# In plain heads of attention, the first addition of probabilities on VectorE instead of GpSimd

## The chip, the core and the metric

The kernel runs on one core of a Trainium2 chip. The metric is the device time of one execution in microseconds. Three runs of the kernel before took 2719.68 to 2723.65 us, with a median of 2723.48. TensorE (PE) does the matmuls, PEld in a profile is its loading of weights, VectorE is DVE, ScalarE is ACT, GpSimd is POOL, and SP issues the transfers.

## What is computed

The input is `x` of 8 x 1024 x 512 numbers in float32. A block of attention with 8 heads of 64 dimensions is followed by a feed-forward block. Cut to what matters:

```
h  = layernorm(x)
q, k = h @ W_qk + b_qk          # per head, interleaved
v  = h @ W_v + b_v
attn = softmax(q k^T * 64**-0.5)
o  = attn @ v
x  = x + (layernorm(o @ W_out + b_out) * gamma + beta + h) * 2**-0.5
x  = x + sigmoid(xr @ W_r^T) * (relu(xk @ W_k^T)**2 @ W_v^T)
```

`xr` and `xk` mix each row of the second layernorm with the row before it. The change concerns the softmax alone: the sum of the exponentials over the keys.

## The kernel before

The first pass (`attention_pass`) works through 8 batches of 8 heads, 64 heads in all, written out head by head; the second pass does the rest from about 1945 us on. A head has 1024 queries and 1024 keys. Keys are taken in 8 tiles of 128 (`TT`). The work of a head `h` is:

- **Scores and exponents.** `scores` (lines 788 to 802) makes for key tile j a block of 128 keys x 1024 queries in one of two areas `ps_st`, ScalarE's `exponent` (617 to 623) writes `probs[:, j, :]` from it. The maximum of each query is subtracted by an extra row in the matmul, so it must be known before the scores.
- **Row maxima.** They are taken a head ahead. `rows` (763 to 781) makes, for head h+1, 16 blocks of 128 queries x 512 keys, j = 0 to 15, in turn in the two areas `ps_max`; VectorE's `reduce_max` (412 to 418) reduces each block and increments `max_done`. Block j may be written only when the maximum of block j-2 has been taken (line 779). `join_max` joins them, `turn_max` (line 786, one per head) turns them into a row.
- **Sums.** The 8 tiles of `probs` are added up in `acc` by seven additions of 128 x 1024 numbers, `add_probs` (314 to 324) on GpSimd: the first is probs 0 + probs 1 (line 320), the other six add one tile each (line 324). Then `sum_rows` (817 to 824) sums over the partitions with a matmul of ones (line 822). It stands at the start of the next head on TensorE, behind `p_at_v` for the last four tiles (line 812) and ahead of `turn_max`.
- **The product with v and the rest.** `p_at_v` (line 812) multiplies probs by v. GpSimd normalises the result and splits it (lines 330 and 335), two heads later, ahead of its additions.
- **Projections** of q and k for the heads to come (`project_qk`, line 739) are put between the blocks above.

Each engine has a list of steps written out by hand, and semaphores between them. Heads differ by their place in the batch (`h % 8`). Places 1 to 5 are plain heads on all engines (place 5 has some more steps on ScalarE and GpSimd), place 0 carries projections of v, places 6 and 7 prepare the next batch. On TensorE, the middle of a plain head is:

```
scores(b, h, 0, 1)
rows(b, h + 1, 3, 4)
scores(b, h, 1, 3)
rows(b, h + 1, 4, 6)
scores(b, h, 3, 4)
rows(b, h + 1, 6, 8)
...
project_qk(b, h + 2, 0, 0, 4)
scores(b, h, 4, 5)
```

and on VectorE the maxima of the next head are taken with the reciprocal of the sums (`invert_sums`) of the head before between them.

Of the kernel before, what the change touches and what calls it, by code (L numbers as in the profile page):

```python
# [19 lines left out]
ALU = mybir.AluOpType  # L20
# [5 lines left out]
HEADS, DH = 8, 64  # L26
KC = C // P
TT = T // P
# [18 lines left out]
def rows_of(j):  # L47

    if j < 8:
        return j % 4, j // 4  # L50
    return 4 + (j - 8) // 2, j % 2


def attention_pass(nc, x, w_qk, b_qk, w_v, b_v, w_out, w_r, spare, stage, o_hi_scratch, o_lo_scratch, inv_scratch, ln1_stats,
                   ident):
    with ExitStack() as ctx:
        def sb(name, shape, dt=F32):
            return ctx.enter_context(nc.sbuf_tensor(name, shape, dt))

        def sem(name):  # L60
            return ctx.enter_context(nc.semaphore(name))
# [18 lines left out]
        probs = sb("probs", [P, TT, T])  # L80
        acc = sb("acc", [P, T])
# [82 lines left out]
        exp_done = sem("exp_done")  # L164
        acc_done = sem("acc_done")
        sum_done = sem("sum_done")
# [27 lines left out]
        with nc.Block() as block:  # L194
# [92 lines left out]
            def _(pool):  # L287
# [9 lines left out]
                def rstd_of(b):  # L297
                    pool.wait_ge(bn_done, b)
                    pool.tensor_tensor(rstd[:, :], mean_var[:, :, 1], eps[:, :], ALU.add).then_inc(eps_done, 1)
                    pool.wait_ge(eps_done, b)  # L300
                    pool.tensor_tensor(shift[:, :], mean_var[:, :, 0], neg_one[:, :], ALU.mult).then_inc(shift_step, 1)
                    pool.tensor_tensor(rstd[:, :], rstd[:, :], neg_half[:, :], ALU.pow).then_inc(rstd_step, 1)
                    pool.wait_ge(shift_step, b)
                    pool.wait_ge(rstd_step, b)
                    pool.tensor_tensor(shift[:, :], shift[:, :], rstd[:, :], ALU.mult).then_inc(rstd_done, 1)
# [8 lines left out]
                def add_probs(b, h, j):  # L314

                    if j == 1:
                        if h >= 1:
                            pool.wait_ge(sum_done, 8 * b + h)
                        pool.wait_ge(exp_done, 64 * b + 8 * h + 2)
                        pool.tensor_tensor(acc[:, :], probs[:, 0, :], probs[:, 1, :], ALU.add).then_inc(acc_done, 1)  # L320
                    else:
                        pool.wait_ge(exp_done, 64 * b + 8 * h + j + 1)
                        pool.wait_ge(acc_done, 56 * b + 7 * h + j - 1)
                        pool.tensor_tensor(acc[:, :], acc[:, :], probs[:, j, :], ALU.add).then_inc(acc_done, 1)  # L324

                def normalise_o(b, h):

                    pool.wait_ge(o_copied, 8 * b + h + 1)
                    pool.wait_ge(inv_in, 256 * b + 32 * h + 32)
                    pool.tensor_tensor(oT[h % 2][:, :], oT[h % 2][:, :], inv_cols[:, :], ALU.mult).then_inc(o_done, 1)  # L330

                def split_o(b, h):

                    pool.wait_ge(oT_hi_done, 8 * b + h + 1)
                    pool.tensor_tensor(oT[h % 2][:, :].bitcast(F32R), oT[h % 2][:, :], oT_hi[h % 2], ALU.subtract).then_inc(oT_lo_done, 1)  # L335
# [10 lines left out]
                def head(b, h, last):  # L346
                    if h >= 2:
                        normalise_o(b, h - 2)
                        split_o(b, h - 2)
                    if h == 5 and not last:  # L350
                        rstd_of(b + 1)
                    for j in range(1, TT):
                        add_probs(b, h, j)

                head(0, 0, False)
                head(0, 1, False)
                for b in range(B - 1):
                    for h in range(2, HEADS + 2):
                        head(b, h, False)
# [7 lines left out]
            def _(dve):  # L367
# [5 lines left out]
                def stats(b, t):  # L373
                    dve.wait_ge(x_in[t // 2], 16 * b + 16)
                    dve.bn_stats(bn6[:, t, :], xb[:, t, :]).then_inc(bn_step, 1)

                def aggregate():
                    for t in range(TT):
                        ins = dve.bn_aggr(mean_var[:, t, :], bn6[:, t, :])
                    ins.then_inc(bn_done, 1)  # L380
# [18 lines left out]
                def store_qk_lo(b, h, half, ps=ps_misc):  # L399
                    dve.wait_ge(qk_hi_done, 16 * b + 2 * h + half + 1)  # L400
                    cols = slice(half * HALF, (half + 1) * HALF)
                    i, hd = h % 2, h % HEADS
                    dve.scalar_tensor_tensor(kA[i][0:DH, cols], ps[DH:P, :], bqk[DH:P, hd:hd + 1],  # L403
                                             f32(kA[i][DH:P, cols]), ALU.add, ALU.subtract).then_inc(k_lo_done, 1)
                    dve.scalar_tensor_tensor(qB[i][0:DH, cols], ps[0:DH, :], bqk[0:DH, hd:hd + 1],
                                             f32(qA[i][0:DH, cols]), ALU.add, ALU.subtract).then_inc(q_lo_done, 1)
# [5 lines left out]
                def reduce_max(b, h, first, end):  # L412

                    for j in range(first, end):
                        r, kh = rows_of(j)
                        dve.wait_ge(rows_done, 128 * b + 16 * h + j + 1)
                        dve.tensor_reduce(half_max[:, r, kh:kh + 1], ps_max[(j + 1) % 2][:, :], AX_X,  # L417
                                          ALU.max).then_inc(max_done, 1)

                def join_max(b, h):  # L420

                    dve.wait_ge(max_done, 128 * b + 16 * h + 16)
                    dve.tensor_reduce(neg_max[:, :], half_max[:, :, :], AX_X, ALU.max, negate=True).then_inc(neg_max_done, 1)

                def invert_sums(b, h):
                    dve.wait_ge(sums_in, 256 * b + 32 * h + 32)
                    dve.reciprocal(inv_sq[:, :], sums_sq[:, :]).then_inc(recip_done, 1)
# [32 lines left out]
                reduce_max(0, 0, 12, 16)  # L460
                join_max(0, 0)

                def plain_head(b, h, last):
                    place = h % HEADS
                    extra = not last
                    if extra and place == 5:
                        dve.wait_ge(bn_step, 8 * b + 16)
                    store_qk_lo(b, h + 1, 0)
                    if extra and 2 <= place <= 4:
                        for t in range(3 * place - 6, min(3 * place - 3, TT)):  # L470
                            stats(b + 1, t)
                    if extra and place == 5:
                        aggregate()
                    reduce_max(b, h + 1, 0, 3)
                    store_qk_lo(b, h + 1, 1)
                    reduce_max(b, h + 1, 3, 4)
                    if h >= 1:
                        invert_sums(b, h - 1)
                    reduce_max(b, h + 1, 4, 16)
                    join_max(b, h + 1)  # L480

                def late_v_head(b, h):
# [53 lines left out]
                def head(b, h, last):  # L536
                    place = h % HEADS
                    if place == 0:
                        late_v_head(b, h)
                    elif place == 6 and not last:  # L540
                        turning_head(b, h)
                    elif place == 7 and not last:
                        early_v_head(b, h)
                    elif place == 7:
                        invert_sums(b, h - 1)
                    else:
                        plain_head(b, h, last)
# [1004 lines left out]
```

## Time and profile before

| | us |
|---|---|
| median of 3 runs | 2723.48 |
| the profiled execution, its time | 2721.03 |
| its span, from the first to the last instruction | 2719.2 |
| PE busy | 2625.8 (97%) |
| PE loads busy | 1782.0 (66%) |
| DVE busy | 1631.3 (60%) |
| POOL busy | 1521.1 (56%) |
| ACT busy | 1290.6 (47%) |

Busy times are unions of the recorded instructions. Matmuls are pipelined and their ends are modelled, so that two of them overlap in the record: what counts is the time from one start to the next. In a row of the time line, like instructions that follow each other closely are merged (x2, x6), and the brackets give the idle time of the engine before the row and what ended it.

### The profile page before, as it was taken

What the parts mean: (1) busy time and instruction counts of PE and PEld (TensorE: products, weight loads), DVE (VectorE), ACT (ScalarE), POOL (GpSimd) and SP (SyncE); (2) the same over time, 40 slices, a digit from 0 to 9 for tenths busy, and PEclk for the clock granted to TensorE, in tenths of its full rate; (3) what the DMA queues carried; (4) which work ended last, traced back from release to release, by engine and by line L of the source; (5) the groups of instructions that cost most, each with busy time, mean ns of one, the idle gap of its engine ahead of it and who ended that gap; (6) DMA issues with size and microseconds to landing.
All of it is one profiled execution on the core that took longest, in us unless ns stands there. A gap on an engine that the chain in (4) does not pass through costs nothing. (4 is left out here: it accounts for less than half of the span.)

```text
span 2719.2 us, 31997 instructions
## 1 busy us (share of the span) xinstructions
PE 2625.8 (97%) x11376; PEld 1782.0 (66%) x11376; DVE 1631.3 (60%) x2679; ACT 1290.6 (47%) x1833; POOL 1521.1 (56%) x819
## 2 busy tenths in 40 slices
PE   6999999999999999999999999999579999999999
PEld 5655656665565666556556666665358888888887
DVE  7555455456545545654554555455278787878785
ACT  3345346335534634553463455344245555555554
POOL 3576477567647756764775676577323333333333
PEclk9999999999999999999999999999779999999999
DMA  2222122122112212211221221122322222222220
GB/s 97 63 47 51 36 78 53 42 71 55 44 38 75 55 40 71 57 42 48 66 55 40 70 60 39 40 50 79 122 90 99 85 96 89 93 92 89 96 77 32
DMA packets 108410, 178.32 MB, mean 66 GB/s; under 512 B 22401, under 2 KB 22913, under 8 KB 108289
## 3 DMA queue, kind: packets, MB, share of 16 engines
q1 hardware_dynamic: 108288, 176.75, 22.5%
q8 instruction: 71, 1.16, 0.2%
q14 instruction: 51, 0.41, 0.0%
HBM read 92.02 MB, written 50.59 MB: 52 GB/s over the span
## 5 line engine op out<-in xcount | busy, mean ns | idle before, releaser
L417 DVE TENSOR_REDUCE half_max<-ps_max 128x1 f32<-128x512 f32 x1024 | 680.3, 687 | 549.7 <-PE ps_max L780 543.4
L324 POOL TENSOR_TENSOR acc<-acc,probs 128x1024 f32<-128x1024 f32 x384 | 914.0, 2380 | 157.5 <-ACT probs L623 109.2
L623 ACT ACTIVATE probs<-ps_st 128x1024 f32<-128x1024 f32 x512 | 522.0, 1023 | 591.8 <-PE ps_st L801 589.6
L812 PE MATMUL ps_o<-probs,v 128*64 128x512 f32 x2048 | 467.7, 598 | 0.0
L800 PE MATMUL ps_st<-qA,kA 128*128 128x512 f32 x1024 | 415.3, 406 | 13.9 <-DMA qB<-max_row 9.4
L801 PE MATMUL ps_st<-qB,kB 65*128 65x512 f32 x1024 | 408.2, 399 | 0.0
L780 PE MATMUL ps_max<-kA,qA 128*128 128x512 f32 x1024 | 386.8, 416 | 3.7 <-issue 1.4
L320 POOL TENSOR_TENSOR acc<-probs 128x1024 f32<-128x1024 f32 x64 | 152.8, 2387 | 287.6 <-ACT probs L623 287.6
L812 PEld LDWEIGHTS ps_o<-probs,v 128*64 128x64 f32 x2048 | 135.6, 136 | 265.4 <-issue 236.5
L780 PEld LDWEIGHTS ps_max<-kA,qA 128*128 128x128 f32 x1024 | 188.6, 188 | 138.6 <-issue 63.5
L800 PEld LDWEIGHTS ps_st<-qA,kA 128*128 128x128 f32 x1024 | 194.7, 190 | 82.3 <-ACT probs L623 32.7
L801 PEld LDWEIGHTS ps_st<-qB,kB 65*128 65x128 f32 x1024 | 194.7, 190 | 40.9
L739 PE MATMUL ps_misc<-xT_hi,wqk_lo 128*128 128x512 f32 x508 | 206.4, 406 | 12.8 <-DVE wqk_lo L450 9.3
L335 POOL TENSOR_TENSOR oT<-oT,spare 128x512 fp32r<-128x512 f32 x64 | 82.3, 1286 | 223.4 <-ACT spare L615 223.4
L739 PE MATMUL ps_misc<-xT_lo,wqk_hi 128*128 128x512 f32 x508 | 201.2, 396 | 0.0
L739 PE MATMUL ps_misc<-xT_hi,wqk_hi 128*128 128x512 f32 x508 | 201.0, 396 | 0.0
L591 ACT ACTIVATE kA<-ps_misc,bqk 64x512 fp32r<-64x512 f32 x127 | 86.6, 682 | 205.1 <-PE ps_misc L739 199.5
L410 DVE TENSOR_TENSOR v<-ps_misc,bv 128x512 f32<-128x512 f32 x60 | 41.5, 692 | 186.0 <-PE ps_misc L748 186.0
L403 DVE SCALAR_TENSOR_TENSOR kA<-ps_misc,bqk,kA 64x512 fp32r<-64x512 f32 x127 | 96.0, 756 | 66.3 <-ACT qA L592 66.0
L1453 PE MATMUL bank<-mix_wout_hi,o_lo 128*128 128x512 f32 x256 | 102.8, 402 | 22.5 <-DMA o_lo<-o_lo_scratch 19.1
L597 ACT ACTIVATE max_row<-ps_max 8x128 fp32r<-8x128 f32 x64 | 17.0, 266 | 225.7 <-PE ps_max L786 225.7
L1212 POOL TENSOR_TENSOR rstd_y<-mv_y,eps 128x4 f32<-128x4 f32 x16 | 3.2, 202 | 205.6 <-DVE mv_y L1257 205.6
(174 smaller groups left out, 4629.6 us busy)
## 6 DMA issues: line engine op xcount, KB each, us to landing
stage<-in_L_attn_x_dram SPq DMA_DIRECT2D x32, 512.0 KB, 5.8
qA<-qA SPq DMA_DIRECT2D x128, 128.0 KB, 2.3
kB<-kA SPq DMA_DIRECT2D x128, 128.0 KB, 2.4
o_hi_scratch<-spare SPq DMA_DIRECT2D x128, 128.0 KB, 2.3
o_lo_scratch<-oT SPq DMA_DIRECT2D x128, 128.0 KB, 2.4
o_hi<-o_hi_scratch SPq DMA_DIRECT2D x16, 1024.0 KB, 5.4
o_lo<-o_lo_scratch SPq DMA_DIRECT2D x16, 1024.0 KB, 7.7
xc<-in_L_attn_x_dram SPq DMA_DIRECT2D x16, 1024.0 KB, 5.2
```

Source lines behind the costliest of these rows:

```text
L320: pool.tensor_tensor(acc[:, :], probs[:, 0, :], probs[:, 1, :], ALU.add).then_inc(acc_done, 1)
L324: pool.tensor_tensor(acc[:, :], acc[:, :], probs[:, j, :], ALU.add).then_inc(acc_done, 1)
L403: dve.scalar_tensor_tensor(kA[i][0:DH, cols], ps[DH:P, :], bqk[DH:P, hd:hd + 1], f32(kA[i][DH:P, cols]), ALU.add, ALU.subtract).then_inc(k ...
L417: dve.tensor_reduce(half_max[:, r, kh:kh + 1], ps_max[(j + 1) % 2][:, :], AX_X, ALU.max).then_inc(max_done, 1)
L591: act.activation(kA[i][DH:P, cols], ps[DH:P, :], ACT.Identity, bias=bqk[DH:P, hd:hd + 1])
L623: act.activation(probs[:, j, :], ps_st[j % 2][:, :], ACT.Exp).then_inc(exp_done, 1)
L739: ins = pe.matmul(ps[:, :], w[:, kc, h % HEADS, :, :].rearrange("p s d -> p (s d)"), xt[:, kc, cols], start=(n == 0), stop=(n == 11))
L780: pe.matmul(ps_max[(j + 1) % 2][:, :], qA[h % 2][:, r * P:(r + 1) * P], kA[h % 2][:, kh * HALF:(kh + 1) * HALF], start=True, stop=True).th ...
L800: pe.matmul(ps_st[j % 2][:, cols], kA[h % 2][:, tile], qA[h % 2][:, cols], start=True, stop=False)
L801: ins = pe.matmul(ps_st[j % 2][:, cols], kB[h % 2][:, tile], qB[h % 2][:, cols], start=False, stop=True)
L812: ins = pe.matmul(ps_o[half * DH:(half + 1) * DH, :], v[:, j, hd * DH:(hd + 1) * DH], probs[:, j, half * HALF:(half + 1) * HALF], start=(j ...
L1453: ins = pe.matmul(out, a[:, kc, a_cols], b[:, kc, b_cols], start=(i == 0), stop=(i == len(prods) - 1))
```

## The change

In heads with place 1 to 5, the first addition of probabilities is taken out of GpSimd's list. VectorE does it, into the same `acc`, behind the row maximum of block 4 (the fifth) of the next head. The increments of `acc_done` stay in the same order, so that GpSimd's second addition waits for VectorE's.

```diff
@@ -349,7 +349,8 @@
                         split_o(b, h - 2)
                     if h == 5 and not last:
                         rstd_of(b + 1)
-                    for j in range(1, TT):
+                    first = 2 if 1 <= h % HEADS <= 5 else 1
+                    for j in range(first, TT):
                         add_probs(b, h, j)
 
                 head(0, 0, False)
@@ -460,6 +461,13 @@
                 reduce_max(0, 0, 12, 16)
                 join_max(0, 0)
 
+                def add_first_probs(b, h):
+
+                    if h >= 1:
+                        dve.wait_ge(sum_done, 8 * b + h)
+                    dve.wait_ge(exp_done, 64 * b + 8 * h + 2)
+                    dve.tensor_tensor(acc[:, :], probs[:, 0, :], probs[:, 1, :], ALU.add).then_inc(acc_done, 1)
+
                 def plain_head(b, h, last):
                     place = h % HEADS
                     extra = not last
@@ -476,7 +484,10 @@
                     reduce_max(b, h + 1, 3, 4)
                     if h >= 1:
                         invert_sums(b, h - 1)
-                    reduce_max(b, h + 1, 4, 16)
+                    reduce_max(b, h + 1, 4, 5)
+                    if 1 <= place <= 5:
+                        add_first_probs(b, h)
+                    reduce_max(b, h + 1, 5, 16)
                     join_max(b, h + 1)
 
                 def late_v_head(b, h):
```

VectorE, one plain head (place 1), from the second half of the projections stored to the joined maximum. Before:

```order
L417 TENSOR_REDUCE half_max<-ps_max 128x1 [waits rows_done] x3
L403 SCALAR_TENSOR_TENSOR kA<-ps_misc,bqk,kA 64x512 [waits qk_hi_done]
L405 SCALAR_TENSOR_TENSOR qB<-ps_misc,bqk,qA 64x512
L417 TENSOR_REDUCE half_max<-ps_max 128x1 [waits rows_done]
L427 RECIPROCAL inv_sq<-sums_sq 32x32 [waits sums_in]
L417 TENSOR_REDUCE half_max<-ps_max 128x1 [waits rows_done] x12
L423 TENSOR_REDUCE neg_max<-half_max 128x8 [waits max_done]
```

The same head now:

```order
L418 TENSOR_REDUCE half_max<-ps_max 128x1 [waits rows_done] x3
L404 SCALAR_TENSOR_TENSOR kA<-ps_misc,bqk,kA 64x512 [waits qk_hi_done]
L406 SCALAR_TENSOR_TENSOR qB<-ps_misc,bqk,qA 64x512
L418 TENSOR_REDUCE half_max<-ps_max 128x1 [waits rows_done]
L428 RECIPROCAL inv_sq<-sums_sq 32x32 [waits sums_in]
L418 TENSOR_REDUCE half_max<-ps_max 128x1 [waits rows_done]
L469 TENSOR_TENSOR acc<-probs 128x1024 [waits exp_done,sum_done]
L418 TENSOR_REDUCE half_max<-ps_max 128x1 [waits rows_done] x11
L424 TENSOR_REDUCE neg_max<-half_max 128x8 [waits max_done]
```

The twelve maxima behind the reciprocal have become one, the addition, and eleven.

GpSimd, two successive plain heads: the addition into `acc` and the normalisation and splitting of an earlier head. Before:

```order
L320 TENSOR_TENSOR acc<-probs 128x1024 [waits exp_done,sum_done]
L324 TENSOR_TENSOR acc<-acc,probs 128x1024 [waits acc_done,exp_done] x6
L330 TENSOR_TENSOR oT<-oT,inv_cols 128x512 [waits inv_in,o_copied]
L335 TENSOR_TENSOR oT<-oT,spare 128x512 [waits oT_hi_done]
L320 TENSOR_TENSOR acc<-probs 128x1024 [waits exp_done,sum_done]
```

Now:

```order
L324 TENSOR_TENSOR acc<-acc,probs 128x1024 [waits acc_done,exp_done] x6
L330 TENSOR_TENSOR oT<-oT,inv_cols 128x512 [waits inv_in,o_copied]
L335 TENSOR_TENSOR oT<-oT,spare 128x512 [waits oT_hi_done]
L324 TENSOR_TENSOR acc<-acc,probs 128x1024 [waits acc_done,exp_done] x6
```

The row of line 320 is gone there, and the six others follow the splitting directly. TensorE's, ScalarE's and SP's lists are the same as before.

## Rows read from the trace of the kernel before

**Rows 1.** The page, busy time of each engine (share of the span).

```profile
PE 2625.8 (97%) x11376; PEld 1782.0 (66%) x11376; DVE 1631.3 (60%) x2679; ACT 1290.6 (47%) x1833; POOL 1521.1 (56%) x819
```

**Rows 2.** Waits: who waited for whom, us in total, times, longest us.

```profile
PEld ps_max L780 <- DVE half_max L417: 35.8, 116, 0.4
...
PE ps_max L822 <- POOL acc L324: 6.3, 2, 4.2
```

**Rows 3.** Time line, PEld, start of a plain head (start, duration, instructions).

```profile
567.31 0.08 PEld L786 LDWEIGHTS ps_max<-ident,neg_max 128*8 128x8 f32 x1 [0.81 <-issue]
```

**Rows 4.** Time line, DVE, the same head.

```profile
573.97 0.67 DVE L417 TENSOR_REDUCE half_max<-ps_max 128x1 f32<-128x512 f32 x1
574.57 0.33 DVE L427 RECIPROCAL inv_sq<-sums_sq 32x32 f32<-32x32 f32 x1
574.91 1.29 DVE L417 TENSOR_REDUCE half_max<-ps_max 128x1 f32<-128x512 f32 x2
576.41 1.29 DVE L417 TENSOR_REDUCE half_max<-ps_max 128x1 f32<-128x512 f32 x2 [0.21 <-PE ps_max L780]
```

**Rows 5.** Time line, PEld, the same head: row products 6 and 7.

```profile
575.75 0.19 PEld L780 LDWEIGHTS ps_max<-kA,qA 128*128 128x128 f32 x1
576.26 0.19 PEld L780 LDWEIGHTS ps_max<-kA,qA 128*128 128x128 f32 x1 [0.32 <-DVE half_max L417]
576.37 0.19 PEld L739 LDWEIGHTS ps_misc<-xT_hi,wqk_lo 128*128 128x128 f32 x1
576.60 0.19 PEld L739 LDWEIGHTS ps_misc<-xT_lo,wqk_hi 128*128 128x128 f32 x1
```

**Rows 6.** Time line, POOL, the same head.

```profile
574.60 2.39 POOL L320 TENSOR_TENSOR acc<-probs 128x1024 f32<-128x1024 f32 x1 [3.87 <-ACT probs L623]
...
577.13 14.98 POOL L324 TENSOR_TENSOR acc<-acc,probs 128x1024 f32<-128x1024 f32 x6
592.08 1.27 POOL L330 TENSOR_TENSOR oT<-oT,inv_cols 128x512 f32<-128x512 f32 x1
```

**Rows 7.** Time line, PEld, where this head ends and the next begins.

```profile
591.49 0.14 PEld L812 LDWEIGHTS ps_o<-probs,v 128*64 128x64 f32 x2 [0.28 <-issue]
592.23 0.26 PEld L822 LDWEIGHTS ps_max<-acc,ones 128*64 128x64 f32 x4 [0.60 <-issue]
593.30 0.08 PEld L786 LDWEIGHTS ps_max<-ident,neg_max 128*8 128x8 f32 x1 [0.81 <-issue]
```

**Rows 8.** Time line, PEld, the end of a head of place 0.

```profile
802.12 0.14 PEld L812 LDWEIGHTS ps_o<-probs,v 128*64 128x64 f32 x2 [0.28 <-issue]
802.55 0.14 PEld L822 LDWEIGHTS ps_max<-acc,ones 128*64 128x64 f32 x2 [0.29 <-issue]
...
803.94 0.08 PEld L786 LDWEIGHTS ps_max<-ident,neg_max 128*8 128x8 f32 x1 [0.81 <-issue]
```

**Rows 9.** Time line, PEld, start and end of a head with a longer gap.

```profile
1828.59 0.08 PEld L786 LDWEIGHTS ps_max<-ident,neg_max 128*8 128x8 f32 x1 [0.81 <-issue]
...
1853.80 0.23 PEld L822 LDWEIGHTS ps_max<-acc,ones 128*64 128x64 f32 x4 [0.89 <-issue]
1854.83 0.08 PEld L786 LDWEIGHTS ps_max<-ident,neg_max 128*8 128x8 f32 x1 [0.81 <-issue]
```

**Rows 10.** Time line, ACT, the head of rows 3 to 7: its first two exponents.

```profile
572.38 2.07 ACT L623 ACTIVATE probs<-ps_st 128x1024 f32<-128x1024 f32 x2
```

**Rows 11.** Groups by line and form, DVE: count, busy us, mean ns, idle before.

```profile
L1292 DVE TENSOR_TENSOR mr_lo<-stage,mr_hi 128x512 fp32r<-128x512 f32 x64 | 40.8, 700 | 0.0
...
L1292 DVE TENSOR_TENSOR mk_lo<-stage,mk_hi 128x512 fp32r<-128x512 f32 x64 | 39.8, 685 | 0.0
...
L1296 DVE TENSOR_TENSOR mix_wout_lo<-stage,mix_wout_hi 128x2048 fp32r<-128x2048 f32 x1 | 2.3, 2292 | 8.6 <-ACT mix_wout_hi L1389 8.6
```

**Rows 12.** One line's instructions, second pass: duration ns min/median/max, first and last start.

```profile
L1286 DVE SCALAR_TENSOR_TENSOR stage<-lnT,mu_r,stage x64: 736/743/1781, 1998.4 to 2685.2; 128x512 f32<-128x512 f32 x64
```

**Rows 13.** Windows: length, busy us (x instructions) by engine, granted clock, DMA share, GB/s.

```profile
1881.00:1907.00 26.00, 23.83 (x100) 13.13 (x98) 12.33 (x20) 11.19 (x14) 19.15 (x10) 1.00 0.18 41
```

## Prediction

> **What bounds the kernel now.** I read the page's busy shares first, then TensorE's waits, and then single heads in the time line. The page shows TensorE busy for 97% of the span and GpSimd for 56% [rows 1]; the reader is to see that the engine which the change relieves is not the full one. TensorE's waits name GpSimd's additions with 6.3 us in 2 waits, and the row maxima of VectorE with 35.8 us in 116 waits of at most 0.4 us [rows 2]. A plain head takes 26.0 us, from the load that turns the maxima at 567.31 to the next at 593.30 [rows 3, 7]. Weights load every 0.23 us in it where nothing waits [rows 5], and the few larger gaps are the subject below.
>
> **Where GpSimd stands in a plain head.** In the head that begins at 567.31 its first addition starts at 574.60, the other six run without a pause from 577.13 for 14.98 us to 592.11, and the next operation starts at 592.08 [rows 6]. The weights for the summing matmuls load at 592.23, which is 0.60 us after the load before it ended, where the page of waits names nothing ("issue") [rows 7]. In a head where GpSimd is long done this gap is 0.29 us [rows 8]. So the load does wait some 0.31 us for the seventh addition. But the matmul behind it does not: from the last load of L812 to the turning load there are 593.30 - 591.49 = 1.81 us in the waiting head and 803.94 - 802.12 = 1.82 us in the other [rows 7, 8]. The array was still busy with earlier matmuls. The cover is thin. In the one head where the gap is 0.89 us, 0.30 us more, the head lasts 1854.83 - 1828.59 = 26.24 us, 0.25 us more than 25.99 [rows 9]. GpSimd is thus about 0.05 us away from being the bound of plain heads, and it bounds none of them but this one. What a shorter GpSimd chain can give in the changed heads is then 0.25 us in all.
>
> **Where VectorE stands at the place of the change.** In the same head VectorE takes row maximum j=3 at 573.97 and the reciprocal at 574.57, then, in a row "x2" of 1.29 us from 574.91, the maxima j=4 and j=5, and in the next "x2" from 576.41 those of j=6 and j=7 [rows 4]. The fifth maximum, behind which the addition is put, is j=4. One maximum lasts 0.69 us, so in a pair of 1.29 the second starts 0.60 us behind the first: j=5 starts at 575.51 and ends at 576.20. TensorE loads the weights of rows(7) at 576.26, 0.06 us later, after 0.32 us put down to a wait for half_max [rows 5]. It is maximum j=5 that it waits for, because ps_max has two banks and row product j wants maximum j-2 (line 779). So **no time is free between maximum j=5 and TensorE**: the first maximum behind the new addition is one on which TensorE waits already, in each plain head.
>
> **The change, part by part.** It touches heads with place 1 to 5, five in each of 8 batches: 40 heads.
>
> 1. The addition put on VectorE. Its wait costs nothing: exp_done wants the second exponent, which ends at 572.38 + 2.07 = 574.45, and VectorE comes by at 575.51 [rows 4, 10]; sum_done is from the head's start. The trace of before has no VectorE addition of 128x1024 in SBUF. Its nearest rows are tensor_tensor of two SBUF inputs: 512 elements take 0.700 and 0.685 us, 2048 take 2.292 [rows 11]. Half of the long one gives 1.15, twice the short one 1.38; a line through both gives 0.692 + 512 x (2.292 - 0.692)/1536 = 1.225 us. I take the line, since the kind is the same and 1024 lies between. The next operation starts some 0.09 us before the end of one (0.69 against 0.60 above), so maximum j=5 comes 1.14 us later, with 1.06 and 1.29 as the ends.
>
> 2. What queues behind it. On VectorE: maximum j=5, then j=6 and j=7; TensorE wants those two only for row products 8 and 9, behind two more groups of projections and scores. On TensorE: rows(7), and behind it in program order all the rest of the head. Since it waits already, every bit of the 1.14 us is lost: projections and scores behind it are not moved ahead of a waiting load. Sum: 40 x 1.14 = **45.6 us** (42.4 to 51.6).
>
> 3. The addition taken from GpSimd. The second addition there now waits for acc_done from VectorE, which comes at 575.51 + 1.23 = 576.74, plus about 0.14 us that GpSimd takes to start behind a release (574.60 against the exponent's end at 574.45) [rows 6, 10]: 576.88 where it was 577.13. So the chain of six ends only 0.25 us sooner, at 591.86. One addition of 2.39 us less in work makes 0.25 us less in time, as the chain starts with the later of the two engines. Meanwhile TensorE reaches the sum 1.14 us later, so the load's wait of 0.31 us goes, and with it the 0.25 us of the one head [rows 7, 9]: **-0.25 us**. No other wait ends on GpSimd's additions in these heads; the wait of 4.2 us [rows 2] belongs to the last heads of the attention, where place is 6 and 7 and nothing is changed.
>
> 4. ScalarE's exponents want acc_done of the head before, which is done; SP's queue has no step moved. GpSimd's small steps for the next batch stand before its additions, where it idles 3.87 us anyhow [rows 6]. The second pass, from about 1945 us on, is untouched. These cost nothing.
>
> Sum: 2721.03 (the profiled execution, 1.83 us over its span of 2719.2) + 45.6 - 0.25 = 2766.4 us. The median of the runs shown, 2723.48, lies 2.45 us above that execution and gives 2768.8; I forecast **2767.5 us**, +1.6%.
>
> **A rule against the row, and the rivals.** In the second pass a VectorE operation of two SBUF inputs has a median of 743 ns and once or more took 1781 [rows 12]: something holds it up for as long as 1.04 us. The Trainium skill ("SBUF — State Buffer", section "Who interferes with whom") says that a VectorE instruction with two SBUF inputs and a GpSimd instruction that reads SBUF exclude each other, and that the one which started first blocks the other. The trace doesn't contradict it; whether it bites here is a question of what GpSimd does from 575.51 to 576.74.
>
> - *Rival A, the lock.* The new addition is held up like the longest of these. Price at most 40 x (1.14 + 1.04) = 87.2 us, time 2810; with a third of that hold-up 2783. Against it: GpSimd idles for 3.87 us ahead of its first addition [rows 6], and in the changed order it goes on idling until VectorE's addition has ended, so there is nothing to collide with. It would need another order than the one written. Chance 0.05.
> - *Rival B, the other side: faster.* GpSimd's chain is the bound. It makes a closed loop: turn to first addition 7.29, to the last one's end 17.51, to the load 0.12, to the next turn 1.07, together 25.99, which is just the period. If TensorE could take the 1.14 us at rows(7) out of slack, the loop would shrink by 0.25 us a head: 40 x 0.25 = 10 us, time 2713.5 (2711.0 by the profiled execution). It decides from the point where at least 1.14 us of slack lies behind rows(7) in the head. For it speaks the exact match of the loop. Against it the match of 1.81 with 1.82 us across two kinds of head, and a matmul every 0.23 us behind rows(7). Chance 0.03.
> - *Rival C, a part is given back.* The 0.31 us at the summing load is real time, and goes when TensorE comes later: 40 x (1.14 - 0.31) = 33.2 us, time 2756. Against it the same match. Chance 0.05.
> - *Rival D, the clock.* A longer stop each head could lower TensorE's clock. Against it: in the stretch 1881 to 1907 TensorE is busy for 23.83 of 26.00 us and the granted clock is 1.00 [rows 13]; the changed head would be busy for all but some 1.2 of 27.1 us. Chance 0.01, far above the range.
>
> **How the numbers follow.** The forecast has 0.86: its ends are 40 x 1.06 and 40 x 1.29 on either time of before, 2763.2 to 2774.8. To leave out no more than 2 in 10 I go down towards rival C and a little up towards the mild form of A: 2758 to 2777. A measurement of this kernel tells about 0.2%, 5.4 us, from no change. Faster has rival B, 0.03; within 0.2% nothing lands but a near cancellation, 0.01; the rest, 0.96, is slower.
>
> **What the profile after would show.** Right: a VectorE addition of 1.2 us x40; the load of rows(7) 1.1 us later with a wait of 1.4 to 1.5 us named half_max, so that this wait grows from 35.8 to some 80 us; a plain head of 27.1 us; GpSimd's second addition at 9.6 us behind the turn (9.82 before), its chain done over 1 us before the summing load, whose gap is back at 0.29. Wrong: heads that still take 26.0 us with the late load (slack that I missed), an addition of over 1.3 us (A), or heads of 26.8 us with the wait at rows(7) in full (C).

## The result, and the profile after

| | before | after |
|---|---|---|
| median, us | 2723.57 (4 runs) | 2767.36 (4 runs) |
| lowest to highest, us | 2719.68 to 2723.98 | 2767.03 to 2767.79 |
| profiled execution, us | 2721.03 | 2767.67 |
| its span, us | 2719.2 | 2765.5 |

The changed kernel takes 1.0166 times as long (95% interval 1.0154 to 1.0178). It is slower by some 44 us. The forecast was 2767.5 us.

The page of the kernel after, busy times first, then one group of GpSimd and one of TensorE whose waits grew. A group's row has the count, busy us, mean ns, idle us before it and what ended that:

```profile
PE 2629.1 (95%) x11376; PEld 1782.6 (64%) x11376; DVE 1677.1 (61%) x2719; ACT 1291.0 (47%) x1833; POOL 1426.7 (52%) x779
...
L324 POOL TENSOR_TENSOR acc<-acc,probs 128x1024 f32<-128x1024 f32 x384 | 914.4, 2381 | 408.1 <-DVE acc L469 237.4
...
L791 PE MATMUL ps_max<-kA,qA 128*128 128x512 f32 x1024 | 391.7, 416 | 44.7 <-DVE half_max L418 40.9
```

TensorE's busy time is what it was, 2629 against 2626 us [rows 1]; its share fell because the span grew. GpSimd lost 94 us of work (40 x 2.39 is 96), and that bought nothing. The matmuls of row products now wait 40.9 us for maxima; the record of before names no wait for half_max at these matmuls, only at their weight loads [rows 2].

The new addition, from the answer on its line (durations in ns min/median/max):

```profile
L469 DVE TENSOR_TENSOR acc<-probs x40: 1215/1215/1217, 102.5 to 1907.3; 128x1024 f32<-128x1024 f32 x40
```

The waits, who waited for whom, us in total, times, longest:

```profile
POOL acc L324 <- DVE acc L469: 237.4, 40, 13.9
...
PEld ps_max L791 <- DVE half_max L418: 81.6, 116, 1.5
...
PE ps_max L791 <- DVE half_max L418: 40.9, 40, 1.1
...
ACT probs L634 <- PE ps_st L812: 634.1, 349, 7.2
```

The wait of weight loads for row maxima went from 35.8 to 81.6 us with the same count of 116 and a longest of 1.5 instead of 0.4 us [rows 2]. Its growth, 45.8 us, is nearly that of the span (46.3 us).

Now one plain head, the same as in [rows 3 to 7], which here begins at 578.96. VectorE, then TensorE's loads at row products 6 and 7:

```profile
585.63 0.67 DVE L418 TENSOR_REDUCE half_max<-ps_max 128x1 f32<-128x512 f32 x1
586.23 0.33 DVE L428 RECIPROCAL inv_sq<-sums_sq 32x32 f32<-32x32 f32 x1
586.56 0.69 DVE L418 TENSOR_REDUCE half_max<-ps_max 128x1 f32<-128x512 f32 x1
587.17 1.22 DVE L469 TENSOR_TENSOR acc<-probs 128x1024 f32<-128x1024 f32 x1
588.30 1.97 DVE L418 TENSOR_REDUCE half_max<-ps_max 128x1 f32<-128x512 f32 x3
```

```profile
587.39 0.19 PEld L791 LDWEIGHTS ps_max<-kA,qA 128*128 128x128 f32 x1
589.04 0.19 PEld L791 LDWEIGHTS ps_max<-kA,qA 128*128 128x128 f32 x1 [1.46 <-DVE half_max L418]
589.15 0.19 PEld L750 LDWEIGHTS ps_misc<-xT_hi,wqk_lo 128*128 128x128 f32 x1
```

Maximum j=5 starts 588.30 - 578.96 = 9.34 us behind the turn, where it started at 8.20 (575.51 - 567.31). The step from the addition to it is 1.13 us. The load of rows(7) stands at 10.08 instead of 8.95 us, 0.05 us behind the end of the maximum as before: its wait went from 0.32 [rows 5] to 1.46 us. GpSimd, and TensorE at the head's end:

```profile
588.53 9.95 POOL L324 TENSOR_TENSOR acc<-acc,probs 128x1024 f32<-128x1024 f32 x4 [6.15 <-DVE acc L469]
599.13 4.89 POOL L324 TENSOR_TENSOR acc<-acc,probs 128x1024 f32<-128x1024 f32 x2 [0.65 <-ACT probs L634]
603.98 1.28 POOL L330 TENSOR_TENSOR oT<-oT,inv_cols 128x512 f32<-128x512 f32 x1
```

```profile
604.69 0.14 PEld L833 LDWEIGHTS ps_max<-acc,ones 128*64 128x64 f32 x2 [0.29 <-issue]
605.12 0.14 PEld L833 LDWEIGHTS ps_max<-acc,ones 128*64 128x64 f32 x2 [0.29 <-issue]
606.08 0.08 PEld L797 LDWEIGHTS ps_max<-ident,neg_max 128*8 128x8 f32 x1 [0.81 <-issue]
```

The head lasts 606.08 - 578.96 = 27.12 us, 1.13 us more than 25.99 [rows 3, 7]. All 40 are alike; two of them have 0.2 us more in both kernels, and the head that took 26.24 us before [rows 9] now takes 27.12 us like the rest. The gap before the summing load is back at 0.29 us.

### The profile page after: what moved, and what is told of

Read it like the earlier page. It is cut to its first block and busy times, and to the rows that moved or that the text cites. A ratio compares the mean times of both kernels' runs of the same rounds, so it can differ in the third digit from the quotient of the medians.

```text
span 2765.5 us, 31997 instructions
## 1 busy us (share of the span) xinstructions
PE 2629.1 (95%) x11376; PEld 1782.6 (64%) x11376; DVE 1677.1 (61%) x2719; ACT 1291.0 (47%) x1833; POOL 1426.7 (52%) x779
## 5 line engine op out<-in xcount | busy, mean ns | idle before, releaser
L791 PE MATMUL ps_max<-kA,qA 128*128 128x512 f32 x1024 | 391.7, 416 | 44.7 <-DVE half_max L418 40.9
L791 PEld LDWEIGHTS ps_max<-kA,qA 128*128 128x128 f32 x1024 | 188.5, 188 | 184.0 <-DVE half_max L418 81.6
L320 POOL TENSOR_TENSOR acc<-probs 128x1024 f32<-128x1024 f32 x24 | 57.4, 2391 | 141.8 <-ACT probs L634 141.8
L750 PEld LDWEIGHTS ps_misc<-xT_hi,wqk_lo 128*128 128x128 f32 x508 | 96.1, 189 | 33.3 <-issue 9.7
```

Source lines behind the costliest of these rows:

```text
L750: ins = pe.matmul(ps[:, :], w[:, kc, h % HEADS, :, :].rearrange("p s d -> p (s d)"), xt[:, kc, cols], start=(n == 0), stop=(n == 11))
L791: pe.matmul(ps_max[(j + 1) % 2][:, :], qA[h % 2][:, r * P:(r + 1) * P], kA[h % 2][:, kh * HALF:(kh + 1) * HALF], start=True, stop=True).th ...
```

## The experiments

The theory to be tested: in plain heads the whole cost is TensorE's stop at rows(7) for maximum j=5, and GpSimd's relief is worth nothing, because TensorE bounds them. Its rivals: an addition on VectorE costs its time wherever it stands (by the handing over of `acc`, or by the reading of `probs`); or part of the relief did count and hides in a greater cost. In the diffs below `...` stands for what is left out; the first two and the last are against the kernel before, the third and the fourth against the change. All medians are of interleaved runs beside the kernel before on the same chip; its medians were 2721.7 us in the first four comparisons, 2720.8 in the next four, 2723.5 in the last. So ratios are what to compare.

### Relief without the delay

```diff
 # GpSimd, head():
+                        if j == 4 and 1 <= h % HEADS <= 5:
+                            continue
                         add_probs(b, h, j)
 # VectorE, plain_head(), from the kernel before:
-                    reduce_max(b, h + 1, 4, 16)
+                    reduce_max(b, h + 1, 4, 10)
+                    if 1 <= place <= 5:
+                        add_fifth_probs(b, h)   # acc + probs 4, waits exp_done and acc_done
+                    reduce_max(b, h + 1, 10, 16)
```

> Relief without the delay: in the same 40 heads VectorE does the fifth of the seven additions (probs 4) behind the tenth row maximum, where it idles 3.9 us, and the first addition stays on GpSimd. Main theory (all of the change's cost is TensorE waiting at rows(7) for maximum j=5, and shorter GpSimd chains are worth nothing in plain heads, which TensorE bounds): plain heads stay at 26.0 us, the gap before the summing load falls from 0.60 to 0.29 us, total 2723.3 us. Rival (the 0.31 us of that gap is real time, hidden in the change's cost): plain heads 25.7 us, 40 x 0.31 = 12 us less, 2711 us. Rival (a handover of acc between GpSimd and VectorE costs the head its own 1.2 us): 2770 us.

Measured: 2721.96 us, ratio 1.0002 (0.9993 to 1.0011). One head, GpSimd and TensorE's end of it; it begins at 1069.18:

```profile
1079.01 4.90 POOL L324 TENSOR_TENSOR acc<-acc,probs 128x1024 f32<-128x1024 f32 x2
1085.38 2.39 POOL L324 TENSOR_TENSOR acc<-acc,probs 128x1024 f32<-128x1024 f32 x1 [1.47 <-DVE acc L469]
1088.22 4.90 POOL L324 TENSOR_TENSOR acc<-acc,probs 128x1024 f32<-128x1024 f32 x2 [0.45 <-ACT probs L634]
1093.07 1.29 POOL L330 TENSOR_TENSOR oT<-oT,inv_cols 128x512 f32<-128x512 f32 x1
```

```profile
1093.79 0.14 PEld L833 LDWEIGHTS ps_max<-acc,ones 128*64 128x64 f32 x2 [0.29 <-issue]
1094.21 0.14 PEld L833 LDWEIGHTS ps_max<-acc,ones 128*64 128x64 f32 x2 [0.29 <-issue]
1095.17 0.08 PEld L797 LDWEIGHTS ps_max<-ident,neg_max 128*8 128x8 f32 x1 [0.81 <-issue]
```

GpSimd's chain ends at 23.9 us behind the turn (1093.12 - 1069.18) instead of 24.8, the gap before the summing load fell to 0.29 us, and the head lasts 25.99 us as before. The same amount of work, 40 additions, was moved to the same engine, `acc` went to and fro once more than in the change, and nothing was lost or gained. That excludes both rivals: the 0.31 us at the load were covered, and here, where no engine that bounds the head waits for it, a handover costs nothing.

### Delay without the relief

```diff
+        unused_max = sb("unused_max", [P, 1])
 ...
-                    reduce_max(b, h + 1, 4, 16)
+                    reduce_max(b, h + 1, 4, 5)
+                    if 1 <= place <= 5:
+                        dve.tensor_reduce(unused_max[:, :], bv[:, :], AX_X, ALU.max)
+                    reduce_max(b, h + 1, 5, 16)
```

> Delay without the relief, and half as much: the kernel before, with an unused VectorE maximum over the 512 numbers of bv behind row maximum j=4 in the 40 heads, which nobody waits for and which reads no probabilities. It moves maximum j=5 by 0.60 us. Main theory: the row products stop TensorE 0.60 us more, plain heads 26.6 us, 40 x 0.60 = 24 us, total 2747.5 us. Rival (the cost comes from the handover of acc, or from reading probs): no change, 2723.5 us. With slack behind rows(7): less than 24 us in proportion.

Measured: 2748.08 us, ratio 1.0097 (1.0082 to 1.0112), that is 26.4 us where 24 were expected. VectorE and the loads of row products 6 and 7 in one head:

```profile
1089.09 0.69 DVE L418 TENSOR_REDUCE half_max<-ps_max 128x1 f32<-128x512 f32 x1
1089.70 0.67 DVE L482 TENSOR_REDUCE unused_max<-bv 128x1 f32<-128x512 f32 x1
1090.29 1.28 DVE L418 TENSOR_REDUCE half_max<-ps_max 128x1 f32<-128x512 f32 x2
```

```profile
1089.90 0.19 PEld L784 LDWEIGHTS ps_max<-kA,qA 128*128 128x128 f32 x1
1091.02 0.19 PEld L784 LDWEIGHTS ps_max<-kA,qA 128*128 128x128 f32 x1 [0.93 <-DVE half_max L418]
```

A step of 0.59 us put in front of maximum j=5 raises the wait from 0.32 to 0.93 us, and the head from 25.99 to 26.58 us. The dose is half of the change's and so is the effect. The operation has nothing to do with probabilities or GpSimd. The 2.8 us beyond 40 x 0.59 = 23.6 lie inside the interval of the ratio (22.3 to 30.5 us). In the profiled executions the 40 heads together grew by 23.3 us, from 1040.2 to 1063.5, and the first plain head began 2.7 us later than in the kernel before (96.59 against 93.85 us), with the same code up to there; the last section comes back to this.

### The addition one maximum later

```diff
-                    reduce_max(b, h + 1, 4, 5)
+                    reduce_max(b, h + 1, 4, 6)
                     if 1 <= place <= 5:
                         add_first_probs(b, h)
-                    reduce_max(b, h + 1, 5, 16)
+                    reduce_max(b, h + 1, 6, 16)
```

> The change with the addition one maximum later, behind j=5 instead of j=4. Main theory: TensorE finds maximum j=5 in time; maxima j=6 and j=7 come 1.1 us later and are just in time for rows(8) and rows(9) (about 0.02 us late for rows(9)); GpSimd's second addition starts 0.35 us later than in the kernel before, which is 0.30 us more than the cover at the summing load: plain heads 26.3 us, 40 x 0.3 = 12 us, total 2735.5 us, with GpSimd's chain now the bound. Rival (an addition on VectorE costs its time in any place of the head): 2767 us as with the change.

Measured: 2736.45 us, ratio 1.0056 (1.0042 to 1.0070). The loads of row products 6 and 7, then GpSimd, then the end of the head, which began at 1077.02:

```profile
1085.96 0.19 PEld L791 LDWEIGHTS ps_max<-kA,qA 128*128 128x128 f32 x1 [0.33 <-DVE half_max L418]
...
1102.28 0.23 PEld L833 LDWEIGHTS ps_max<-acc,ones 128*64 128x64 f32 x4 [0.94 <-issue]
1103.32 0.08 PEld L797 LDWEIGHTS ps_max<-ident,neg_max 128*8 128x8 f32 x1 [0.81 <-issue]
```

```profile
1087.19 14.98 POOL L324 TENSOR_TENSOR acc<-acc,probs 128x1024 f32<-128x1024 f32 x6 [6.75 <-DVE acc L469]
```

The stop at rows(7) is the old one, 0.33 us. GpSimd's second addition starts at 10.17 us behind the turn where it was 9.82, and the gap before the summing load grew from 0.60 to 0.94 us. The head takes 26.30 us, 0.31 more: by these rows GpSimd's chain is the bound this time. No run took GpSimd's part away to prove it. Moved by a single maximum, the same addition costs a third, and for another reason.

### The change, with TensorE coming later to rows(7)

```diff
-                    rows(b, h + 1, 6, 8)
+                    rows(b, h + 1, 6, 7)
 ...
                         project_qk(b, h + 2, 0, 0, 4)
+                    rows(b, h + 1, 7, 8)
                     scores(b, h, 4, 5)
```

> The change as it is, with TensorE's order in plain heads altered by one step: rows(7) stands behind the four projection matmuls instead of ahead of them. Main theory: maximum j=5 is as late as with the change (about 10.03 us behind the turn), but TensorE arrives at rows(7) at 9.8 us instead of 8.9, so it stops some 0.35 us instead of 1.3; against the kernel before, which stops 0.16 us there, 40 x 0.2 = 8 us, total 2731 us. Rival (cost lies elsewhere than at rows(7)): still 2767 us.

Measured: 2729.96 us, ratio 1.0035 (1.0021 to 1.0049). The head begins at 1073.78 and the next at 1099.97, 26.19 us. The addition starts at 8.21 us as in the change:

```profile
1081.99 1.21 DVE L469 TENSOR_TENSOR acc<-probs 128x1024 f32<-128x1024 f32 x1
1083.12 0.68 DVE L418 TENSOR_REDUCE half_max<-ps_max 128x1 f32<-128x512 f32 x1
```

```profile
1083.86 0.19 PEld L791 LDWEIGHTS ps_max<-kA,qA 128*128 128x128 f32 x1 [0.54 <-DVE half_max L418]
```

The maximum is as late as ever, and with one step of TensorE's list moved some 36 of 45 us are back, by the two ratios. VectorE and GpSimd have the change's lists. So the cost lies in the wait, at this step. What is left is 0.2 us a head: the load of rows(7) still waits 0.54 us, where it waited 0.32 before.

### That order, without and with the relief

The step of the last run was applied to the kernel before, and to the kernel of the relief run.

> The kernel before with TensorE's order of the last run (rows(7) behind the four projection matmuls), all additions on GpSimd. TensorE loses its 0.16 us stop at rows(7) in plain heads. Main theory: GpSimd's loop (turn, first addition, seven additions, summing load, turn) is only 0.05 us shorter than TensorE's own time, so that the head shrinks by 0.05 us alone and the gap before the summing load grows: 40 x 0.05 = 2 us, 2720 to 2721.5 us, within noise of before. Rival (GpSimd is nowhere near the bound): 40 x 0.16 = 6 us, 2716.5 us.

> The same order of TensorE, with the fifth addition on VectorE behind the tenth row maximum as in the relief run. Main theory: now GpSimd's chain has 0.6 us to spare, and the 0.16 us come out: plain heads 25.84 us, total 2723.3 - 6.2 = 2717 us. Rival (relief worth nothing under any order): same as the run before it.

Measured: without the relief 2720.94 us, ratio 1.0001 (0.9992 to 1.0010); with it 2717.60 us, ratio 0.9988 (0.9979 to 0.9997). In one head without it, TensorE's last load of probs times v and the summing load:

```profile
1093.54 0.14 PEld L812 LDWEIGHTS ps_o<-probs,v 128*64 128x64 f32 x2 [0.28 <-issue]
1094.48 0.23 PEld L822 LDWEIGHTS ps_max<-acc,ones 128*64 128x64 f32 x4 [0.80 <-issue]
```

TensorE saved 0.16 us at rows(7), of which 0.02 came out (the head lasts 25.97 us); the rest went into the gap, 0.80 us instead of 0.60. With the relief the gap is 0.28 us and the head 25.83 us, so there all of it came out. The prediction's remark that GpSimd is only about 0.05 us away from being the bound is borne out by this pair. Relief is worth nothing in the old order; in this one the 40 heads together take 1033.5 us instead of 1039.5, so that it is worth 6.0 us by the heads. The two medians lie only 3.3 us apart and the intervals of the two ratios overlap, so the reading rests on the heads and not on the totals.

### An order of TensorE meant to wait on nothing just issued

```diff
                     scores(b, h, 0, 1)
                     rows(b, h + 1, 3, 4)
-                    scores(b, h, 1, 3)
-                    rows(b, h + 1, 4, 6)
-                    scores(b, h, 3, 4)
-                    rows(b, h + 1, 6, 8)
+                    scores(b, h, 1, 2)
+                    rows(b, h + 1, 4, 5)
+                    scores(b, h, 2, 3)
                     more = not (last and h == HEADS - 2)
                     if more:
                         free_of_qk(b, h + 1, 1)
                         project_qk(b, h + 2, 0, 0, 4)
+                    scores(b, h, 3, 4)
+                    rows(b, h + 1, 5, 7)
                     scores(b, h, 4, 5)
-                    rows(b, h + 1, 8, 10)
+                    rows(b, h + 1, 7, 8)
                     scores(b, h, 5, 6)
+                    rows(b, h + 1, 8, 10)
                     p_at_v(b, h, 0)
```

It was run with the relief, with all additions on GpSimd, and with the change itself.

> A version meant to beat both: the relief at the free place, and an order of TensorE in plain heads in which no step waits on work just issued: scores 1, rows 4, scores 2, four projections, scores 3, rows 5 and 6, scores 4, rows 7, scores 5, rows 8 and 9, probs times v. It takes out the three stops in a plain head of before (0.21 us at scores 2, 0.08 at rows 5, 0.16 at rows 7). Main theory: plain heads 25.55 to 25.6 us, 40 x 0.4 = 16 us, total 2707 us. If a maximum or an exponent comes late in the new order: a part of that.

> That order of TensorE alone, with all seven additions on GpSimd. Main theory: GpSimd's loop bounds plain heads at about 25.94 us whatever TensorE saves: total 2720 to 2721.5 us, so that the relief is worth 14 us here and nothing in the order of before. Rival (TensorE's order alone decides): 2707 us like the run before it.

> The change itself (first addition on VectorE behind maximum j=4), with the full order of TensorE of the two runs before. Main theory (the change costs only by whom it makes wait): in this order row product 5 ends at 9.35 us behind the turn, so that maximum j=5 isn't ready to be taken before 9.6, and the addition from 8.05 to 9.3 fits in the gap: no stop at rows(7). GpSimd's chain ends at about 24.4 us, its load at 24.5 against 24.56 that TensorE's cover allows, so it is just in time: plain heads 25.63 us, total 2708 us, 59 us less than the change in its own order. If GpSimd's chain starts later than that: up to 25.75 us a head, 2713 us. Rival (an addition at this place costs its time, whatever the order): 2708 + 45 = 2753 us.

| TensorE's new order with | us | ratio (interval) | plain head, us (median of 40) |
|---|---|---|---|
| the relief (fifth addition on VectorE) | 2708.42 | 0.9953 (0.9940 to 0.9967) | 25.63 |
| all additions on GpSimd | 2720.83 | 0.9999 (0.9990 to 1.0008) | 25.95 |
| the change (first addition on VectorE) | 2711.71 | 0.9959 (0.9945 to 0.9972) | 25.63 |

Waits of weight loads for row maxima, in the relief's run and in that of the change:

```profile
PEld ps_max L791 <- DVE half_max L419: 11.9, 33, 0.4
```

```profile
PEld ps_max L791 <- DVE half_max L418: 11.8, 32, 0.4
```

And one head of the run with the change, which began at 1062.74: VectorE's addition, GpSimd, and TensorE at the head's end.

```profile
1070.81 1.20 DVE L469 TENSOR_TENSOR acc<-probs 128x1024 f32<-128x1024 f32 x1
```

```profile
1072.15 15.01 POOL L324 TENSOR_TENSOR acc<-acc,probs 128x1024 f32<-128x1024 f32 x6 [5.99 <-DVE acc L469]
```

```profile
1087.27 0.29 PEld L833 LDWEIGHTS ps_max<-acc,ones 128*64 128x64 f32 x4 [0.57 <-issue]
1088.37 0.08 PEld L797 LDWEIGHTS ps_max<-ident,neg_max 128*8 128x8 f32 x1 [0.81 <-issue]
```

The stop at rows(7) is gone: 11.8 us of waits for maxima in the whole kernel, none of them over 0.4 us. The addition of the change stands at the same place in VectorE's list, and costs nothing, because TensorE doesn't want maximum j=5 before it is done. The order alone, without relief, gives nothing (the head takes 25.95 us, where 25.94 was expected of GpSimd's loop, and the relief alone takes it to 25.63). Order and relief together give a kernel faster than both, by 0.47% against before and some 2% against the change. The gain of 0.36 us a head is a little under the 0.4 expected. The change's own relief leaves a gap of 0.57 us at the summing load, so it is at the edge of GpSimd's bound: three of its 40 heads take 0.2 us more than the same heads in the relief's run. The fifth addition gives more room.

In the relief's run the last head of place 6 also got 0.6 us longer, 26.50 us instead of 25.90. The order is not the reason, since the other two runs with it have 25.88 and 25.91 us there. The granted clock is, by this window at the head's end (length, busy us by engine, granted clock, DMA share, GB/s):

```profile
1891.60:1892.80 1.20, 1.20 (x4) 0.00 (x0) 0.00 (x0) 0.00 (x0) 0.68 (x1) 0.50 0.00 0
```

In the 2.50 us before it fell (1889.00 to 1891.50) TensorE was busy for 0.30 us. In the other two runs it is 1.00 over the last 1.2 us of this head.

## Why the prediction was right

- *TensorE is the bound, and GpSimd's wait is covered* (the 1.81 against 1.82 us): right. The relief run left the time as it was, and moved the gap to 0.29 us.
- *Maximum j=5 is wanted at once*: right. The profile after shows the load of rows(7) 1.13 us later, and 40 more waits at the matmul.
- *The price of the addition*: 1.225 us by the line between two forms, 1.215 measured; the step 1.13 for 1.14. Half of the long form was 5% too low and twice the short one 14% too high; the line through two sizes of the same operation was within 1%.
- *The sum*: 45.6 - 0.25. In the two profiled executions the stretch from the first plain head's turn to the last head's turn grew from 1906.91 - 93.85 = 1813.06 to 1952.14 - 94.26 = 1857.88 us, by 44.8; 40 x 1.13 - 0.25 is 44.95. Of the span's growth another 0.4 us lie before and 1.0 behind that stretch, where the code is unchanged. That the forecast of 2767.5 lies only 0.14 us from the median is in part luck: it was chosen between 2766.4 and 2768.8, and the runs of the kernel before spread over more than that (2719.68 to 2723.98 us).
- *The rule of two SBUF inputs* (the Trainium skill, "SBUF — State Buffer", section "Who interferes with whom") has it that a VectorE instruction with two SBUF inputs and a GpSimd instruction that reads SBUF lock each other out, the later one waiting. It didn't bite at the new additions: all 40 lasted 1215 to 1217 ns, and GpSimd ran nothing during any of them. In the second pass, where the code is unchanged, the same trace agrees with it. There a VectorE subtraction of two SBUF tensors starts 0.31 us behind a GpSimd addition, takes 1.52 us and ends 0.54 us behind it; with GpSimd idle the same subtraction takes 0.69 us:

```profile
2108.09 1.29 POOL L1228 TENSOR_TENSOR xc<-xc,bet 128x512 f32<-128x512 f32 x1
```

```profile
2108.40 1.52 DVE L1285 TENSOR_TENSOR act_lo<-sq,act_hi 128x512 fp32r<-128x512 f32 x1 [1.67 <-ACT sq L1420]
...
2151.60 0.69 DVE L1285 TENSOR_TENSOR act_lo<-sq,act_hi 128x512 fp32r<-128x512 f32 x1 [3.19 <-ACT sq L1420]
```

So being held up, as in rival A, does happen to VectorE in this kernel, by 0.83 us in this case; the new addition escaped it by the order in which the two engines work, as the prediction argued. No run puts a VectorE addition of probabilities beside a GpSimd one.

- **A step that failed, with no effect on the time**: GpSimd's chain was to end 0.25 us sooner than before, and over 1 us before the summing load. It ended at 25.06 us behind the turn, later than the 24.81 of before, and 0.67 us before the load. Its second addition did start when forecast (9.57 us). But the sixth of the seven, which wants the exponent of tile 6, waited 0.65 us for ScalarE instead of the usual 0.14. I had put the exponents down as costing nothing, since they want only what is done; I left out that ScalarE itself waits for scores, which came 1.13 us later with all of TensorE's list. In the run in which TensorE is late by 0.2 us only, six additions run through in 14.96 us:

```profile
1083.35 14.96 POOL L324 TENSOR_TENSOR acc<-acc,probs 128x1024 f32<-128x1024 f32 x6 [6.16 <-DVE acc L469]
```

- *Rivals.* B (faster, by GpSimd's loop) and C (0.31 us given back) are both refuted by the relief run; the exact match of GpSimd's loop with the period was no evidence for B, because its parts run from one turn to the next without a hole and so add up to the period whoever bounds it. That GpSimd stands right behind TensorE is shown by the single head of 26.24 us and by the runs with the other orders. A and D didn't occur: the granted clock is 1.00 in the changed head:

```profile
578.90:606.10 27.20, 26.12 (x112) 15.55 (x111) 16.79 (x26) 12.56 (x16) 16.79 (x8) 1.00 0.43 126
```

## What to carry to other kernels

Before moving work to an engine that is half idle, ask who waits for the next thing in its list: VectorE idled 40% of the time, and yet at that place each 0.1 us on it was 0.1 us of TensorE, while behind the tenth maximum a whole addition was free. Price such a move by the step from the new operation to the next one and count it in full if the bounding engine already loses time there. A wait of a weight load alone doesn't show that: the one of 0.31 us at the sum was covered by matmuls still queued, and of the 0.32 us at rows(7) only 0.16 came out when it was taken away. When two engines' loops are within a few hundredths of each other, neither relief nor a better order shows anything alone; try them together.

## What the runs showed that was not expected

Kernels with the same code up to there reach their first plain head at different times: at 93.80 us in the relief's run with the new order, and at 97.17 us in that of the change. Windows of these two executions (length, busy us by engine, granted clock, DMA share, GB/s):

```profile
56.00:66.00 10.00, 9.17 (x38) 7.03 (x39) 6.54 (x10) 4.93 (x6) 2.23 (x1) 1.00 0.24 53
```

```profile
56.00:66.00 10.00, 8.70 (x25) 6.48 (x24) 4.28 (x7) 2.54 (x4) 0.00 (x0) 0.66 0.12 27
```

In the second, TensorE's granted clock is 0.66 over these 10 us, a mix of its full level of 2.4 GHz and of half of it, 1.2 GHz; in the first it is 1.00. The clock fell at 56.6 us. TensorE had been nearly idle since 54.5 us, but in the first execution it was so too, since 53.9 us, and kept its clock. The second execution's window stands first:

```profile
54.50:56.60 2.10, 0.28 (x2) 0.08 (x1) 2.03 (x4) 1.30 (x3) 0.00 (x0) 0.99 0.00 0
```

```profile
53.90:56.60 2.70, 0.27 (x1) 0.08 (x1) 2.60 (x5) 1.26 (x3) 0.00 (x0) 1.00 0.21 45
```

All eleven profiled executions fall in two groups. The first plain head begins at 93.8 to 94.3 us in the four in which the clock doesn't fall there (the kernel before and the changed one are among them), and at 96.4 to 97.3 us in the seven in which it falls at 56.6 to 58.0 us for 3.4 or 6.8 us. The two executions above took 2708.51 and 2711.36 us. The second starts its plain heads 3.37 us later, and the first loses 0.6 us in the last head of place 6; that gives 2.8 of the 2.85 us between them. The runs of the kernel before spread over 6.0 us (2718.4 to 2724.4 over all comparisons), so this is about half of their spread. What decides between the two groups was not tried. For the comparisons it means that a difference under some 3 us should be read from the heads, not from one execution's total.
